# A delta-rule scan inside a two-layer network: how each chunk's triangular matrix is inverted, and in what order its work is issued

## What is computed

```python
v_scaled, wk_scaled = v * beta, wk * beta
cum = jnp.cumsum(log_decay, -1)                       # within a chunk
L_mask = jnp.tril(jnp.exp(jnp.tril(cum[..., :, None] - cum[..., None, :])))
M = jnp.tril(-(wk_scaled @ jnp.swapaxes(wk, -1, -2)) * L_mask, -1)
A = solve_triangular(eye - M, eye, lower=True, unit_diagonal=True)
intra = jnp.tril(rk @ jnp.swapaxes(wk, -1, -2) * L_mask, -1)
...
def step(S, inp):                                     # over the chunks
    v_new = A_i @ vsc_i - A_i @ wkd_i @ S
    o_i = rkd_i @ S + intra_i @ v_new
    S = ced_i * S + wkp_i @ v_new
```

## Time and profile before

| | us |
|---|---|
| median of 3 runs | 2764.56 (2763.82 to 2767.65) |
| span of the profiled execution | 2801.9 |
| TensorE busy, share of the span | 2532.3 (90%) |
| VectorE | 1974.3 (70%) |
| ScalarE | 1662.8 (59%) |
| GpSimd | 1187.3 (42%) |
| first matmul of the second stage, in the profiled execution | 504.03 |

### The profile page before, as it was taken

The page is one execution under the profiler, slowest core; times in us unless marked ns, Lnnn a source line. Parts: engine busy times, 40 slices in busy tenths (PEclk is TensorE's granted clock), DMA queues, the critical chain, the costliest instruction groups (busy, mean ns, idle before and its releaser), DMA issues.

```text
span 2801.9 us, 40990 instructions
## 1 busy us (share of the span) xinstructions
PE 2532.3 (90%) x14724; PEld 2088.8 (75%) x14724; DVE 1974.3 (70%) x3028; ACT 1662.8 (59%) x2586; POOL 1187.3 (42%) x758
## 2 busy tenths in 40 slices
PE   6999989999999997996997988979979889899797
PEld 5989889899999996884666766657666666676676
DVE  6776656566666664677858768688687686886877
ACT  5555444444444443666675776676666766766664
POOL 2225553000000005315646656566556655565675
PEclk9999999999999998998999999999999989999998
DMA  4564453444444434524544544455445445454553
GB/s 145 200 207 136 146 165 129 140 142 142 142 141 141 142 126 134 164 84 151 188 145 141 175 159 152 150 166 175 142 143 196 156 153 158 154 167 148 158 177 124
DMA packets 229610, 427.60 MB, mean 153 GB/s; under 512 B 24898, under 2 KB 112642, under 8 KB 229395
## 3 DMA queue, kind: packets, MB, share of 16 engines
q1 hardware_dynamic: 223250, 407.98, 44.7%
q0 software_dynamic: 6144, 16.79, 1.8%
HBM read 347.58 MB, written 77.10 MB: 152 GB/s over the span
## 4 chain that ended last, share of the span: by engine, by line
PE 62%; DVE 14%; ACT 11%; issue 8%; POOL 2%; DMA 1%; another core or an unknown queue 1%; DVEq 0%; POOLq 0%; SPq 0%; ACTq 0%
PE pb L1350 12%; PE pb L1328 12%; DVE pb L1814 7%; PE pb L820 6%; PE pb L2123 5%; PE pb L2118 4%; PE pb L2042 3%; PE pb L2017 3%; ACT L1945 2%; PE pb L2033 2%; DVE UU L1820 2%; PE pb L2061 2%; ACT pb L1945 2%; PE pb L2086 2%; PE pb L812 2%
## 5 line engine op out<-in xcount | busy, mean ns | idle before, releaser
L1746 POOL TENSOR_TENSOR UU<-dx,BB 128x1024 f32<-128x1024 f32 x256 | 609.0, 2393 | 438.8 <-PE pb L2017 438.1
L1945 ACT ACTIVATE pb<-dt,al 128x512 f32<-128x512 f32 x512 | 341.5, 686 | 188.1 <-DVE UU L1820 186.9
L1814 DVE TENSOR_TENSOR_SCAN pb<-pb,hs,UU 128x512 f32<-128x512 f32 x256 | 328.6, 1284 | 106.4 <-ACT pb L1945 91.5
L1814 DVE TENSOR_TENSOR_SCAN pb<-pb,UU 128x512 f32<-128x512 f32 x256 | 313.0, 1223 | 125.4 <-ACT pb L1945 119.2
L1255 DVE TENSOR_TENSOR HL<-HF,HH 128x512 fp32r<-128x512 f32 x248 | 171.6, 692 | 300.3 <-ACT HH L1170 275.9
L1166 ACT ACTIVATE HF<-pb,BU 128x512 f32<-128x512 f32 x248 | 171.0, 689 | 347.3 <-PE pb L1328 318.4
L1820 DVE TENSOR_TENSOR UU<-pb,CC 128x512 f32<-128x512 f32 x512 | 351.4, 686 | 26.8 <-DMA CC<-bcd 9.2
L2118 PE MATMUL pb<-HAh,WH 128*128 128x512 f32 x1024 | 276.0, 409 | 29.3 <-ACT HAh L1983 21.9
L1129 POOL DMA_INDIRECT ya<-yg,sl x32 | 35.7, 1115 | 624.2 <-DMA yg<-YO 562.7
L2017 PEld LDWEIGHTS pb<-ident,UU 128*128 128x128 f32 x2048 | 240.7, 144 | 76.6 <-issue 48.6
L1350 PE MATMUL pb<-W2h,HH 128*128 128x256 f32 x992 | 287.7, 290 | 5.7 <-issue 5.7
(11 more groups left out here) (301 smaller groups left out, 5267.5 us busy)
## 6 DMA issues: line engine op xcount, KB each, us to landing
WH<-fhd SPq DMA_DIRECT2D x176, 512.0 KB, 3.3
BB<-bcd SPq DMA_DIRECT2D x256, 256.0 KB, 4.6
CC<-bcd SPq DMA_DIRECT2D x256, 256.0 KB, 4.8
raw<-in_w1a SPq DMA_DIRECT2D x23, 1024.0 KB, 5.0
raw<-in_w2a SPq DMA_DIRECT2D x23, 1024.0 KB, 7.7
xg<-zt SPq DMA_DIRECT2D x23, 512.0 KB, 6.1
TM<-xg SPq DMA_DIRECT2D x23, 512.0 KB, 8.7
yg<-YO SPq DMA_DIRECT2D x23, 512.0 KB, 3.1
```

The lines of the kernel that those rows point to most:

```text
L1746: e.tensor_tensor(ubuf(n)[:], dx[p][:], BB[n % 4][:].rearrange("p (a m) -> p a m", a=1).to_broadcast([P, 2, 512]), ALU.mult).then_inc(p_u. ...
L1814: e.tensor_tensor_scan(h_[:], h_[:], uu[:, c, :], first, ALU.mult, ALU.add).then_inc(v_sc.sem, 1)
L1945: e.activation(abank(n, c)[:], dt[p][:, c, :], ACT.Exp, scale=al1[:, 2 * p + c, s:s + 1]).then_inc(c_a.sem, 1)
```

## The change

The inverse starts from diagonal blocks of 16. Of M, now in the tile M2 for both heads, SyncE stores the eight diagonal blocks to DRAM (`md`), waits for them, and loads them back as MB, in which each group of 16 partitions holds its block's 15 rows. VectorE solves all blocks at once by forward substitution: `solve` is a copy and 15 pairs of a multiply and an add, each waiting for the one before. `inverse` spreads the result over the diagonal as DT, TensorE transposes it (d4), ScalarE copies it to Dm, and levels 4 to 6 follow. Levels 1 to 3 and the seed are gone.

The work of a chunk is issued in another order: the next chunk's kk, M, blocks, v and kq stand in this chunk, and the rows of the chunk after the next are turned in it. Decay limits are taken by ScalarE (`lower`, `upper`: Relu with a bias) rather than VectorE. The copies W1h and W2h stand behind the last chunk.

```diff
-        order = ["kq", "P1", "t1", "D1", "v", "P2", "t2", "D2", "wkT", "P3", "t3", "D3", "wkS", "P4", "t4", "D4",
-                 "P5", "t5", "D5", "P6", "t6", "T6", "vn", "rkT'", "o", "kk'", "S", "MT'"]
+        ahead = ["rkT", "z", "kk", "MT", "v", "kq", "rkT'"]
+        order = ["kk'", "wkT", "d4", "wkS", "P4", "D4", "P5", "t5", "D5", "P6", "t6", "T6", "MT'", "vn", "rkT''", "v'", "o", "S", "kq'"]
...
+            def blocks(n):
+                for h in range(2):
+                    e.wait_ge(*g_dve[h].at("M", n))
+                for q in range(8):
+                    e.dma_start(md[n, 16 * q:16 * q + 16], M2[16 * q:16 * q + 16, :, :, 16 * q:16 * q + 16]).then_inc(s_md, 16)
+                e.wait_ge(s_md, 128 * (n + 1))
+                if n:
+                    e.wait_ge(*g_x.at(30, n - 1))
+                for q in range(8):
+                    e.dma_start(MB[16 * q:16 * q + 16].rearrange("p r g c -> p (r g c)"),
+                                md[n, 16 * q + 1:16 * q + 16].rearrange("(o r) h b c -> o (r h b c)", o=1).to_broadcast([16, 1920])).then_inc(s_mb, 16)
...
+            blocks(0)
             for n in range(NSEQ):
-                if 1 <= n < NSEQ - 1:
-                    sums(n + 1)
+                if n + 1 < NSEQ:
+                    blocks(n + 1)
+                if n + 2 < NSEQ:
+                    sums(n + 2)
+                if n:
+                    residuals(n - 1)
...
+            def solve(n, steps):
+                for k in steps:
+                    r = (k - 1) // 2
+                    if k == 0:
+                        e.wait_ge(s_mb, 128 * (n + 1))
...
+                        e.tensor_copy(X16[:], eye[:].rearrange("p (a r) -> p a r", a=1).to_broadcast([P, 8, 16])).then_inc(g_x.sem, 1)
+                        continue
+                    e.wait_ge(*g_x.at(k - 1, n))
+                    if k % 2:
+                        e.tensor_tensor(Y16[:, :, r:15], MB[:, r:15, :, r].rearrange("p r g -> p g r"),
+                                        X16[:, :, r:r + 1].to_broadcast([P, 8, 15 - r]), ALU.mult).then_inc(g_x.sem, 1)
+                    else:
+                        e.tensor_tensor(X16[:, :, r + 1:16], X16[:, :, r + 1:16], Y16[:, :, r:15], ALU.add).then_inc(g_x.sem, 1)
...
             for n in range(NSEQ):
...
+                more = n + 1 < NSEQ
+                copy("wk", n, "wkT", "wk")
+                copy("d4", n, "d4", "Dm")
+                high(3 * n)
+                if more:
+                    upper(n + 1)
+                    decays(n + 1, "ET")
+                    decays(n + 1, "ez")
+                    carried(n + 1)
+                rest(3 * n)
...
+                copy("t5", n, "t5", "DT")
+                high(3 * n + 1)
+                copy("t6", n, "t6", "DT")
+                if more:
+                    copy("MT", n + 1, "MT", "MT")
+                rest(3 * n + 1)
                 copy("vn", n, "vn", "vn")
...
+                if n + 2 < NSEQ:
+                    turned_rows(n + 2)
+                high(3 * n + 2)
+                if n + 2 < NSEQ:
+                    lower(n + 2)
```

More of the change, by code:

```diff
@@ L602, in dve_a, with level @@
                     (2, 1): 10, (2, 2): 11, (2, 3): 12, (2, 4): 13}
-            decay(0)
             for h in range(2):
                 mix(0, h)
-                seed(0, h)
-            for n in range(NSEQ):
+            norms(1)
+            for h in range(2):
+                values(0, h)
+            for h in range(2):
+                inner(0, h)
+            solve(0, range(31))
+            for h in range(2):
+                inverse(0, h)
+            def level(l, n):
                 for h in range(2):
@@ new lines, in routed @@
+            def routed(n, l):
+                if (n, l) in PART:
+                    route(PART[n, l])
+            for n in range(NSEQ):
+                more = n + 1 < NSEQ
+                if n:
+                    residual_a(n - 1)
+                if more:
+                    for h in range(2):
+                        mix(n + 1, h)
+                routed(n, 1)
+                for h in range(2):
+                    W, bk = TB[h], four(gbank("wkS", n, h))
+                    e.wait_ge(*g_pe[h].at("wkS", n))
+                    e.wait_ge(*g_dve[h].at("vs", n))
+                    for b in range(4):
+                        t = e.scalar_tensor_tensor(out=W["vsc"][:, b, :], in0=bk[:, b, :], scalar=sm["bec"][:, n + 8 * b, h:h + 1],
+                                                   in1=W["vsc"][:, b, :], op0=ALU.mult, op1=ALU.add)
+                    t.then_inc(g_dve[h].sem, 1)
+                routed(n, 2)
+                for l in (4, 5, 6):
+                    level(l, n)
+                    routed(n, l - 1)
@@ L667, in dve_a @@
                     t.then_inc(g_dve[h].sem, 1)
[L668 to L675 removed]
+                if more:
+                    solve(n + 1, range(12, 31))
+                    for h in range(2):
+                        inverse(n + 1, h)
+                    for h in range(2):
+                        inner(n + 1, h)
+            residual_a(NSEQ - 1)
             e.wait_ge(s_cnt, NCH)
@@ new lines, in sums_of, with await_sums, lower @@
+            def sums_of(n, h):
+                return ZR[h] if n else gbank("z", 0, h)[:].rearrange("p (b m) -> p b m", b=4)
+            def await_sums(n, h):
+                if n:
+                    e.wait_ge(s_zr, 16 + 32 * n)
+                else:
+                    e.wait_ge(*g_pe[h].at("z", 0))
+            def lower(n):
+                for h in range(2):
+                    W, z_ = TB[h], sums_of(n, h)
+                    await_sums(n, h)
+                    if n:
+                        e.wait_ge(*g_dve[h].at("M", n - 1))
+                    for b in range(4):
+                        t = e.activation(W["E"][:, b, :], z_[:, b, :], ACT.Relu, bias=sm["ncum"][:, n + 8 * b, h:h + 1])
+                    t.then_inc(g_act[h].sem, 1)
@@ new lines, in roots, with high, rest @@
+            def roots(n):
+                e.wait_ge(s_sq, 8 * n + 8)
+                e.activation(rn[:, n:NT:8, :], rn[:, n:NT:8, :], ACT.Sqrt).then_inc(s_rnq, 1)
+            def high(c):
+                if c < NCH:
+                    e.wait_ge(s_craw, 16 * (c + 1))
+                    if c:
+                        e.wait_ge(s_cst, 32 * c)
+                    e.activation(chi[:], craw[:], ACT.Copy).then_inc(s_chi, 1)
+            def rest(c):
+                if c < NCH:
+                    e.wait_ge(s_clo, c + 1)
+                    e.activation(craw[:], clo[:].bitcast(F32), ACT.Abs, accum_out=cnt[:, c:c + 1]).then_inc(s_cnt, 1)
```

413 lines of the change are left out of this document (223 added, 190 removed).

## The result

The changed kernel takes 2859.1 us (median of 4 runs, 2854.7 to 2861.2) where the kernel before took 2765.2 on the same chip: 1.0342 times as long, 95% interval 1.0328 to 1.0357. The forecast had the sign and the mechanism, 2788 us, and too narrow a range. The first matmul of the second stage starts at 572.68 us instead of 504.03.

What follows compares the result with a forecast made beforehand. TensorE was taken to bound the kernel before, the chunk loop (60.5 us) the changed one. Start, chunks and end summed to 527.9 us against 504.0; the 23.9 more, added to 2764.56, gave about 2788, range 2695 to 2835.

Steps and rivals of the forecast that it cites:

- the mechanism: Chunk loop through SyncE's transfers, ScalarE's t6 and the solver sets the pace, 60.5 us against 56.1; TensorE waits for t6.
- d4 of chunk 0: Start of the sum: M at 60.7, block round trip to 72.0, then solver, inverse and contention, giving 82 us.
- T6 to the next M: Second half of the chunk loop, through TensorE products and VectorE's solver: 27.5 us, with contention 31.5.
- Chain A: First half of the chunk loop, M to T6 through stores, MB loads, ZR, craw, chi and t6: 29.0 us.
- MB's bytes: Loads of the diagonal blocks: 983 KB at 331 GB/s in 3.0 us, ending with their issues; bounds 3.0 or 22.
- rival C: MB loads move at ZR's 44 GB/s, adding 19 us to each of 8 round trips: about 2940; chance 0.07.
- The contention: Solver steps on VectorE held up by GpSimd's SBUF operations: 4 us a chunk taken, between 0 and 8.7.
- B: As a chain, T6 to the next M: 27.5 us, 31.5 with contention; elsewhere short for Rival B.
- The clock: TensorE's v-path products after idling at T6 run at a lowered clock: 9.0 us becomes 11.2, 2.2 more.
- The end: Chunk 7 from d4 to the second stage, with W copies and GpSimd subtractions behind it: 34.7 us.
- Rival B: Transfers behind ZR do not wait for it, so the loop opens: 2725, or 2697 without contention; chance 0.22.
- rival D: TensorE stays the bound at 37.5 us a chunk, so the saving arrives in full: 2640; chance 0.03.

Runs made afterwards that it cites:

- e_all_late: Changed kernel with blocks, ZR loads and sd stores issued behind the load of the second weight piece; 2819.1 us, 1.0060 times the kernel before.
- e_nosolve: Changed kernel with 29 of the 31 solver steps left out, all transfers and waits kept; 2786.5 us, 1.0097 times the kernel before.
- e_warm: Changed kernel with 120 filler products on TensorE ahead of T6's wait; 2980.7 us, 1.0625 times the kernel before.
- e_zr_actq: Changed kernel with the ZR loads issued by ScalarE into its own queue; 2851.8 us, 1.0329 times the kernel before.
- e_best2: Changed kernel with blocks, ZR, sd behind second weight piece, ZR in 2 KB runs, W1h/W2h copies beside level 6; 2745.0 us, 0.9951 times the kernel before.
- e_best3: e_best2 with ScalarE's OT copies put ahead of the third chi and of lower; 2734.1 us, 0.9904 times the kernel before.
- b_again2: The kernel before with no edit, profiled again in a single run; 2764.7 us, first stage 486.2 us.
- b_flat: The kernel before with ZR read in runs of 2 KB instead of four rows of 512 bytes; 2749.7 us, 0.9963 times the kernel before.

## Why the prediction was wrong, point by point

**What failed is the sum, and the base it was added to.** The terms of the loop and of its two ends were too small by 44.8 us: the first stage ends at 572.7, not 527.9. Then the difference was added to a median of 2764.56, on whose kind of chip the first stage of the kernel before ends at 486.2, not at the 504.0 that was subtracted: 17.9 us. Of the 70.6 us by which 2859.1 lies above the forecast, 3.4 came behind the first stage and 4.5 lie within what single runs differ.

**The mechanism stood.** The chunk is a loop, M to T6 through SyncE, ZR and craw, and T6 to M through TensorE and the solver; TensorE is no longer the bound. e_all_late removes the first half and T6 comes at once; e_nosolve takes 11.0 us from the second and 9.6 arrive. Chi idles 16 to 22 us in the middle of chunks 0 to 5, T6 waits for t6, the clock is 0.50 there, and chunk 6 is 12 us shorter than chunk 5. Each of these was named ahead. One part is read from the order on ScalarE and was not tried by itself: no run moves only the second chi behind t6, which would be the smallest repair. The sizes below were not right, and all of them were too small:

| term | forecast | measured |
|---|---|---|
| d4 of chunk 0 | 82 | 87.4 |
| M to T6, chunks 0, 1, 2 | 27.6, 29.0, 31.4 | 29.9, 31.3, 33.3 |
| the same, chunks 3, 4, 5 | 29.0 each | 30.3, 33.3, 31.8 |
| the same, chunk 6 | 18.5 | 23.0 |
| T6 to the next M, chunks 0 to 5 | 31.5 each | 35.2, 36.1, 33.2, 33.6, 32.4, 32.6 |
| d4 of chunk 7 to the second stage | 34.7 | 41.6 |
| first stage | 527.9 | 572.7 |

- **Chain A, stores and issues.** The eight stores were priced by sd's 0.45 us an issue; they take 0.63 each (5.06), and with the landing 6.4 instead of 5.1. The MB issues take 3.6 instead of 3.2. From the ZR issue to chi are 21.56 us in chunk 2, forecast 21.5 with the rows tiles; that this agrees is in part luck, for the MB bytes that the forecast had landed by then still fill the engines at ZR's issue (share 0.93 at 119 GB/s from 232 to 238). The whole chain came out 1 to 5 us short. In chunks 4 to 6, where it is most short, 1 to 2 us of that stand behind the last MB issue; what takes them is left open.
- **MB's bytes.** "They take 983 KB / 331 GB/s = 3.0 and end about with them" failed. In chunk 0, where nothing else moves much, MB lands 9.4 us after its first issue (66.90 to 76.33), 5.9 after the last. Timelines of SyncE and VectorE:

```profile
66.90 3.58 SPq L307 DMA_DIRECT2D MB<-md  x8
...
76.33 0.23 DVE L553 COPY X<-eye 128x128 f32<-128x128 f32 x1 [6.50 <-DMA MB<-md]
```

The windows view of the same stretch:

```profile
66.90:70.50 3.60, 2.01 (x19) 1.77 (x17) 2.92 (x5) 3.35 (x18) 0.00 (x0) 1.00 0.84 137
70.50:73.50 3.00, 2.53 (x14) 2.56 (x15) 0.00 (x0) 3.00 (x10) 0.00 (x0) 0.68 1.05 128
```

  The engines are full at 128 GB/s. MB takes 9.4 us where the start of the sum had 6.2, and the stores 6.5 instead of 5.1; the solver starts at 76.33, not 72.0, which is 4.3 of the 5.4 us at the start. MB's price lies between the two bounds given (3 and 22), and it is rival C in small: C wanted 19 us a chunk.
- **The solver.** The copy and 30 steps alone were forecast at 7.9 us and take 8.4 with nothing beside them (e_all_late). The contention was the mis-sized term: 4 us forecast, between 0 and 8.7; the steps of the solves for chunks 1 to 6 take 12.7 to 13.5 us busy against 7.5, so 5.2 to 6.0. The rule cited there (the Trainium skill, "SBUF — State Buffer", section "SBUF: two separate sides") holds in the rows above, where each long step ends with a GpSimd operation; but there the copy, with one SBUF input, is held up as well (2.06 us instead of 0.22), where the forecast counted only the thirty steps with two. The 8.7 is not reached: from the copy's start GpSimd works 7.8 us beside this solve (clo, the four on E, two rkdT), in these 7.8 us seven steps end that take 2.0 us undisturbed, and 5.8 are lost. The forecast took a value near the middle, while all of these fall beside the solver. In chunks 0 and 1 VectorE's routing stands inside the solver too (L618 from 140.3 to 142.5, L644 to L649 from 207.8 to 209.9), 2 us each that no term of B held; that is most of what the 35.2 and 36.1 of the table lie above the other chunks.
- **The clock** was forecast at 2.2 us a chunk, a value picked inside a range; e_warm shows 2.2.
- **The end** was short by 6.9: the wkS product stands between d4 and P4 (2 us, left out of the sum), and 5.4 us pass from GpSimd's last subtraction to the second stage where 0.4 was taken.
- **The base.** The forecast added a difference to a median of 2764.56 that was read from a trace of 2801.9. That gap of 37 was passed over as a constant; 18 us of it lay in the very stage that changes. On the kind of chip of the median the first stage ends at 486, so even a perfect sum of 572.7 would have given 2764.6 + 68.7 = 2833; with 86.6 it is 2851, and 2859 was measured.
- **The range** was drawn from the spread of T and the stores alone. T came at 65.6 in the mean of chunks 1 to 5 (from d4 to d4), inside its 56 to 66. The range's end, 2835, had no room for the start, the end and the base, each of which erred by 5 to 18 us to the same side. **Rival B** and **rival D** did not occur. B hung on the loads behind ZR getting through, and in e_zr_actq they do not even from another queue.

## What to carry to other kernels

When an engine's instruction stream mixes a side job with the main chain, the side job's wait becomes the chain's: here one copy between t5 and t6 tied TensorE to a DMA backlog, and moving transfers and copies by a few places, with ZR read in longer runs, was worth as much as the 13.8 us of TensorE work a chunk that the new algorithm saves (66.2 to 51.5 us a chunk from the changed kernel to e_best2). Work taken off the bounding engine pays only as far as the next loop is open, and after each repair one has to look where the wait has gone: it went from the second piece to the third, and in e_best3 TensorE waits 3.02 us at d4 (285.06) for VectorE's operations right behind the solver. If the profiled execution is longer than the median, find out in which stage it is before its numbers are used as a base.

## What the runs showed of the hardware

- A load of 128 partitions x four rows of 512 bytes (256 KB, the same rows for all partitions) lands 10.1 us after its issue in the median (b_again2), and 3.6 us when the four rows are one run of 2 KB (b_flat, same chip). While two such loads of rows run, the DMA engines show a share of 0.26 to 0.28 and still take little else.
- Loads of 7.7 KB runs into 16 partitions at a time fill the DMA engines (share 1.05) at 128 GB/s, where weight pieces move at 331 to 338; whether the few partitions or the repeated reads do that, no run tells. A store of 64-byte pieces from SBUF to DRAM costs SyncE 0.63 us an issue, also at 89.23, where nothing had been issued for 18 us, against 0.33 to 0.50 for the issues in the earlier trace rows. Behind a backlog any issue can take longer: three xg stores take 9.71 us at 240.68 in the changed kernel and 2.58 at 208.71.
- A VectorE operation of 0.3 us that meets a GpSimd operation on SBUF ends 0.1 us after it, up to 2.06 us for a copy that takes 0.22 alone. One VectorE operation ends with each GpSimd operation, so a chain of short ones lost 5.8 us beside 7.8 us of GpSimd.
- One program's first stage can differ by 18 us of 504 between chips, with its other stages differing by 20 to 30 us, while the first stage of the changed kernel differs by 1 us (572.8 and 574.0).
